# Four q offsets per load, 16 snapshot places, and node n at partition n/25 in a graph network on one Trainium2 core

## The chip, the cores and the metric

The program runs on one core of one Trainium2 chip as a single launch. The metric is device time in microseconds (us). TensorE (PE in the profile, PEld its weight loads), VectorE (DVE), ScalarE (ACT), GpSimd (POOL) and SyncE (SP) have instruction queues of their own and meet at semaphores. Three runs of the kernel before gave 8099.27, 8096.51 and 8084.9 us, median 8096.51.

## The reference

N = 3125 nodes with 128 features, E = 100,000 directed edges sorted by `dst`. Four stages, each added to its input and normalised:

```python
def _transformer_conv(x, src, dst, qw, qb, kw, kb, vw, vb, sw, sb):      # 8 heads of 16
    q, k, v = x@qw+qb, x@kw+kb, x@vw+vb                                   # (N, 8, 16)
    alpha = sum(q[dst] * k[src], -1) / sqrt(16)
    a = exp(alpha - segment_max(alpha, dst)[dst])
    a = a / segment_sum(a, dst)[dst]
    return segment_sum(v[src] * a[:, :, None], dst) + x @ sw + sb

L0: conv(relu(conv(x)))                                     # two such layers
L1: mean = segment_sum(x[dst], src) / max(deg(src), 1);  out = [x, mean] @ W.T + b
L2: h = x@W_enc; three times: m = relu(h[src] + ea) * edge_atten; sum by dst; two-layer MLP
L3: h = x@W.T + b; z = (h@a1)[src] + (h@a2)[dst]
    h' = segment_sum(exp(-leaky_relu(z, 0.2)) * h[dst], src); layernorm; elu
x = layernorm(x + Lk(x))   for each of the four
```

`deg(src)` is the number of edges with that source, and both sums of L1 and L3 go by `src`, against the order of the edges.

## The kernel before, in words

Node tensors live in SBUF as 128 partitions by 25 slots of 128 features (NT = 25, NP = 3200). Before the change node n sits at partition n % 128, slot n // 128.

**Preparation** (to about 163 us) makes lists: which node window each batch of edges belongs to, where each node's last partial sum stands (`last_item`), and for each source node which rows of the counting table it needs (`own_at`, from one-column products in line 504).

**conv_edges**, lines 595 to 830, runs once for each of the two layers of L0 (263 to 1747 us and 1961 to 3404 us). It has 208 batches a layer; a batch is 4 groups of 128 edges. It is software-pipelined: the iteration of batch t asks for the q rows of batch t+1 and finishes batch t-10 (`BEHIND`). On each engine a batch has:
- POOL: 4 gathers of k and v rows by edge (L622), into a ring of `SLOTS` places.
- PE: `ask`, which reads the q rows as a product of one-hot matrices with the q table in SBUF, 12 bf16 products (L696). Where in the q table each half of the batch starts is a number that PE reads from SBUF into a register first (`value_load`, L692), once for each half. Then `tally`, 704 counting products a layer (L702, up to four a batch), each added into PSUM bank 7; and the item products (L740), fp32, which sum weighted v rows and weights of batch t-10, two items of two products each.
- DVE: q times k (L783), v times weights (L788), head sums (L793), the weighted one-hot matrices (L796), evacuation of the items (L819), one-hot matrices for counting (L767, L772); every eighth batch the scans (L804 to L810).
- ACT: a snapshot (L661) of bank 7 after each tally, since each running count is wanted on its own, and a copy of the weights into the batch's `va` (L682), which the item products wait for.
- SP: writes the snapshots to `snap_tab` in DRAM, four at a time, and the items to `item_tab`.

A tally waits for the snapshot of the one before. PE's order in an iteration is tally, ask (load, six products, load, six products), tally, item, tally, item, tally; the last is followed by the first tally of the next iteration. ACT takes the first two snapshots of an iteration, then L682, then the other two.

**by_src**, lines 1447 to 1500, forms the sums by source for L1 (`x`, 3502 to 3726 us) and L3 (attention, 7730 to 8008 us). For each of 25 slots n of destination nodes POOL gathers two rows per partition of `snap_tab` (L1459, 128 x 3200 fp32, the count up to the end of a node's edges and the count up to its start), DVE subtracts them (L1468), in L1 sums them to in-degrees (L1477), in L3 takes the smaller of two exponentials (L1471) that ACT computes (L1487, L1489) and multiplies (L1474). PE then adds 25 products (L1496) with the counts as stationary operand and the features moving, 128 columns each, which leaves the sums node by partition.

**The rest**: GINE (L2's three layers, 3869 to 7656 us) is untouched. Linear layers go through `node_linear`. x comes in by two transfers (L208 24 slots, L210 the last 53 nodes), the output leaves by two more (L1598, L1599).

## Time and profile before

| | |
|---|---|
| runs | 8099.27, 8096.51, 8084.9 us |
| profiled execution, its own time | 8076.82 us |
| its span in the trace | 8075.1 us |
| mean granted PE clock | 0.591 |
| conv_edges, two layers | 1484.0 + 1443.0 us |
| by_src mean, by_src attention | 224 + 278 us |
| GINE | 3787 us |

The profile's page gives busy times by engine and by line; the windows view gives them for a stretch; the timeline lists instructions in order, with the idle time of the engine ahead of each in brackets and what ended it; the waits view sums those idle times. The granted clock is a share of the full 2.4 GHz.

### The profile page before, as it was taken

Reading aid. Unit: us, or ns where it says so; the run is one execution under the profiler, and the core shown is the slowest. Engines: PE = TensorE matmul, PEld = TensorE weight load, DVE = VectorE, ACT = ScalarE, POOL = GpSimd, SP = SyncE. Lnnn points to the kernel's source line nnn. Section 1 sums busy time; section 2 is a strip of 40 time slices with the busy share of each in tenths; the row PEclk is TensorE's granted clock in tenths of the full one; section 3 lists DMA queues with packets and bytes.
Section 4 is the critical chain, followed back from the end, with each engine's and each line's share of the span. In section 5 each row is a group of like instructions: output and inputs, shape, how many; then the busy total and the mean of one; then the engine's idle time right before and its main releaser. Section 6 shows DMA issues by size and latency. Waiting matters only on the chain. (4 is left out here: it accounts for less than half of the span.)

```text
span 8075.1 us, 75499 instructions
## 1 busy us (share of the span) xinstructions
PE 3659.2 (45%) x15737; PEld 2363.8 (29%) x15739; DVE 4330.2 (54%) x9443; ACT 866.8 (11%) x2809; POOL 4213.9 (52%) x4279
## 2 busy tenths in 40 slices
PE   4366666663666666655222322332322323322244
PEld 2254444442444444455110101111110101100144
DVE  5455555554555555576444444344444344544478
ACT  0011111110111111101000000000000000000043
POOL 0455555533555555410566666466666466666443
PEclk7555555565555555577556555565566665566677
DMA  1454555524555454364322222222222222222264
GB/s 30 138 147 141 145 149 145 146 79 122 149 145 145 142 148 140 109 258 168 100 85 87 88 85 87 69 89 85 87 87 85 70 87 85 90 86 87 65 238 187
DMA packets 571997, 943.76 MB, mean 117 GB/s; under 512 B 90581, under 2 KB 413611, under 8 KB 558680
## 3 DMA queue, kind: packets, MB, share of 16 engines
q0 software_dynamic: 173728, 545.15, 22.4%
q1 hardware_dynamic: 398008, 395.34, 15.7%
q8 instruction: 139, 2.28, 0.1%
q14 instruction: 122, 1.00, 0.0%
HBM read 619.47 MB, written 320.66 MB: 116 GB/s over the span
## 5 line engine op out<-in xcount | busy, mean ns | idle before, releaser
L1199 POOL DMA_INDIRECT big<-h_tab,big x2352 | 2237.8, 951 | 1420.0 <-issue 799.3
L622 POOL DMA_INDIRECT big<-kv_tab,big x1664 | 1617.4, 972 | 1330.7 <-DVE big L788 867.6
L1235 PE MATMUL psum<-big 128*128 128x512 f32 x1176 | 969.8, 973 | 2505.4 <-DVE big L1263 2062.1
L1256 DVE SCALAR_TENSOR_TENSOR big<-big 128x128 f32<-128x128 f32 x2352 | 827.2, 352 | 1274.0 <-issue 1233.8
L1235 PEld LDWEIGHTS psum<-big 128*128 128x128 f32 x1176 | 308.5, 290 | 3013.9 <-issue 2253.8
L740 PE MATMUL psum<-big 128*128 128x136 f32 x3328 | 931.4, 433 | 488.8 <-issue 417.1
L740 PEld LDWEIGHTS psum<-big 128*128 128x128 f32 x3328 | 781.9, 315 | 642.2 <-issue 605.1
L696 PE MATMUL psum<-big 128*128 x4992 | 713.3, 296 | 408.9 <-issue 408.7
L1268 DVE TENSOR_SCALAR big<-big 128x128 f32<-128x128 f32 x2352 | 718.0, 306 | 311.3 <-issue 261.8
L783 DVE TENSOR_TENSOR big<-psum,big 128x512 f32<-128x512 f32 x416 | 287.5, 691 | 851.9 <-PE psum L696 554.9
L702 PE MATMUL psum<-big 128*128 128x128 bf16 x1408 | 577.7, 410 | 216.1 <-ACT big L661 112.6
L696 PEld LDWEIGHTS psum<-big 128*128 128x128 bf16 x4992 | 454.2, 120 | 711.6 <-issue 671.7
L661 ACT COPY big<-psum 125x128 f32<-125x128 f32 x1408 | 376.3, 267 | 2444.5 <-PE psum L702 1517.0
L1263 DVE TENSOR_TENSOR big<-psum,big 128x512 f32<-128x512 f32 x588 | 404.3, 688 | 299.7 <-issue 199.7
L1220 ACT COPY big<-psum 128x128 f32<-128x128 f32 x294 | 77.9, 265 | 3312.5 <-issue 1555.2
L1459 POOL DMA_INDIRECT big<-snap_tab,small x100 | 215.3, 2153 | 397.1 <-DVE big L1468 218.3
L819 DVE SCALAR_TENSOR_TENSOR big<-big,psum 128x136 f32<-128x136 f32 x832 | 294.5, 354 | 204.0 <-PE psum L740 81.7
L702 PEld LDWEIGHTS psum<-big 128*128 128x128 bf16 x1408 | 227.4, 161 | 306.8 <-issue 258.5
L788 DVE TENSOR_TENSOR big<-big 128x512 f32<-128x512 f32 x416 | 284.1, 683 | 0.5 <-ACT big L669 0.5
L796 DVE TENSOR_TENSOR big<-big,small 128x512 f32<-128x512 f32 x416 | 284.2, 683 | 0.0
L793 DVE TENSOR_REDUCE big<-big 128x32 f32<-128x512 f32 x416 | 282.8, 680 | 0.7
L1496 PE MATMUL psum<-skip,big 128*128 128x128 f32 x1250 | 183.7, 320 | 110.3 <-DVE big L1474 110.3
(374 smaller groups left out, 3359.9 us busy)
## 6 DMA issues: line engine op xcount, KB each, us to landing
run_tab<-big SPq DMA_DIRECT2D x294, 512.0 KB
snap_tab<-big SPq DMA_DIRECT2D x352, 224.0 KB
item_tab<-big SPq DMA_DIRECT2D x208, 272.0 KB
big<-loc_tab SPq DMA_DIRECT2D x104, 512.0 KB
big<-h_tab,big POOLq DMA_INDIRECT x2352
big<-kv_tab,big POOLq DMA_INDIRECT x1664
snap_tab<-big SPq DMA_DIRECT2D x352, 26.0 KB
kv_tab<-big SPq DMA_DIRECT2D x10, 640.0 KB, 3.3
```

What stands on the lines that cost most here:

```text
L622: nc.gpsimd.indirect_dma_start(out=kv[:, b % SLOTS, k, :], out_offset=None, in_=kv_tab, in_offset=bass.IndirectOffsetOnAxis(ap=src_item[:, ...
L661: nc.scalar.copy(snaps[0:125, n % 8 * P:(n % 8 + 1) * P], bank[7][0:125, 0:P]).then_inc(snapped, 1)
L696: ins_ = nc.tensor.matmul(bank[b % 2][:, k * P:(k + 1) * P], hot_T[b // 4 % 2][:, (b % 4 * 4 + k) * P:(b % 4 * 4 + k + 1) * P], q3[:, bass ...
L702: nc.tensor.matmul(bank[7][:, 0:P], key_hot[n // 8 % 2][:, n % 8::8], lo_hot[n // 8 % 2][:, n % 8::8], start=first_c + n == 0, stop=True, ...
L740: ins_ = nc.tensor.matmul(region(2 * b + i), hot[b % 2][:, k * P:(k + 1) * P], va[b % 2][:, k, :], start=s == 0, stop=s == 1)
L783: nc.vector.tensor_tensor(prod[t % 2].rearrange("p (k c) -> p k c", c=D), bank[t % 2][:, :].rearrange("p (k c) -> p k c", c=D), kv[:, t % ...
L819: nc.vector.scalar_tensor_tensor(run[:, i % 8, :], run[:, (i - 1) % 8, :], keep[:, i:i + 1], region(i), ALU.mult, ALU.add).then_inc(run_do ...
L1199: nc.gpsimd.indirect_dma_start(out=ring[:, slot * D:(slot + 1) * D], out_offset=None, in_=h_tab, in_offset=bass.IndirectOffsetOnAxis(ap=sr ...
L1235: nc.tensor.matmul(bank[2 * u + k][:, :], ea_T[u], w_blocks[:, k * 512:(k + 1) * 512], start=True, stop=True).then_inc(mm_done, 1)
L1256: nc.vector.scalar_tensor_tensor(run[:, slot * D:(slot + 1) * D], run[:, (slot - 1) % RUN * D:((slot - 1) % RUN + 1) * D], same_nat[:, bas ...
L1263: nc.vector.tensor_tensor(z_of(u), bank[u][:, :], ring[:, u * 512:(u + 1) * 512], ALU.add).then_inc(z_done, 1)
L1268: nc.vector.tensor_scalar(m_of(u)[:, k * D:(k + 1) * D], z_of(u)[:, k * D:(k + 1) * D], 0.0, weight_nat[:, bass.ds(16 * i + 4 * u + k, 1)] ...
```

## The change

1. PE reads four q offsets at once, once in two batches (L702), without the bounds instructions, and applies them as offsets of a slice.
2. PE's order is tally, half of ask, tally, other half of ask, tally, item, tally, item.
3. `snaps` has 16 places for 8, is written out eight at a time; `SLOTS` is 14 for 15.
4. Node n is at partition n // 25, slot n % 25. A partition's 25 nodes are neighbours in DRAM: tables are written and read as rows of one partition, x and out as 96 + 29 partitions of 12.8 KB. The lists are made to match.
5. In this layout the count up to the start of a node in slot n is the count up to the end of its neighbour in the slot before; `own_at` has 30 columns and by_src makes 30 gathers for 50, into nine buffers.
6. by_src's products are turned: features stationary, counts moving, 512 columns at a time, seven for 25. A new `turn_back` brings the sums back to node by partition (25 products, 25 DVE operations, after copies from PSUM by ACT and DVE). L1's linear part on x moves ahead of by_src, the part on the mean goes into `turn_back`.
7. In L1 the subtraction also sums (one DVE pass for two). In L3 DVE takes the smaller exponent ahead of one Exp on ACT, and the product takes `min(…, 3e38)` in the same pass.

```diff
-SLOTS = 15
+SLOTS = 14
-        snaps = take(8 * P)
+        snaps = take(16 * P)
-        own_at = small[:, 330:330 + 2 * NT].bitcast(I32)
+        own_at = small[:, 330:330 + NT + 5].bitcast(I32)
         def table(t, cols=None):
-            return t.rearrange("(t p) c -> p t c", p=P)
+            return t.rearrange("(p t) c -> p t c", t=NT)
...
-                    sp.dma_start(x3[:, 0:NT - 1, :], a["x"][0:(NT - 1) * P, :].rearrange("(t p) d -> p t d", p=P)).then_inc(loads, 16)
+                    rows = a["x"].rearrange("(p t) d -> p (t d)", t=NT)
+                    sp.dma_start(x[0:96, :], rows[0:96, :]).then_inc(loads, 16)
                     sp.wait_ge(cleared, 1)
-                    sp.dma_start(x3[0:TAIL, NT - 1, :], a["x"][(NT - 1) * P:N, :]).then_inc(loads, 16)
+                    sp.dma_start(x[96:NODES_P, :], rows[96:NODES_P, :]).then_inc(loads, 16)
...
-                        def ask(b):
-                            pe.wait_ge(hotT_done, b // 4 + 1)
-                            later(pe, prod_done, b - 1)
-                            for i in range(2):
-                                at = nc.tensor.value_load(q_at[0:1, 2 * b + i:2 * b + i + 1], min_val=0, max_val=(NWIN - 1) * 3 * D)
+                        def windows_of(b):
+                            return nc.values_load_multi_w_load_instructions(q_at[0:1, 2 * b:2 * b + 4], engines=(mybir.EngineType.PE,), min_val=0, max_val=(NWIN - 1) * 3 * D,
+                                                                            skip_runtime_bounds_check_because="the list of windows is capped when it is made")[1]
+                        def ask(b, i, at):
...
                             if t + 1 < BATCHES:
-                                ask(t + 1)
+                                ask(t + 1, 0, at[(t + 1) % 2 * 2])
                             for n in turn[1:2]:
                                 tally(n)
+                            if t + 1 < BATCHES:
+                                ask(t + 1, 1, at[(t + 1) % 2 * 2 + 1])
...
+                            for n in turn[2:3]:
+                                tally(n)
                             b = t - BEHIND
...
                                     if i == 0:
-                                        for n in turn[2:3]:
+                                        for n in turn[3:]:
                                             tally(n)
-                            for n in turn[2 if b < 0 else 3:]:
-                                tally(n)
+                            if t % 2 == 0 and t + 2 < BATCHES:
+                                at = windows_of(t + 2)
...
-                        for n in range(NT):
-                            later(pool, diff, n - 1)
-                            for k, rows in enumerate((upto_own, upto_last)):
-                                nc.gpsimd.indirect_dma_start(out=rows[n % 2], out_offset=None, in_=snap_tab,
+                        for v in range(NT + 5):
+                            later(pool, mm_done, v - R + 1)
+                            at = NT + v if v < 5 else v - 5
+                            nc.gpsimd.indirect_dma_start(out=counts[v % R], out_offset=None, in_=snap_tab,
...
-                            for a_ in range(NT):
-                                ins_ = nc.tensor.matmul(bank[a_ // 4][:, (a_ % 4) * D:(a_ % 4 + 1) * D], own[n % 3][:, a_ * P:(a_ + 1) * P], feat[:, n * D:(n + 1) * D],
+                            for lo in range(0, NP, 512):
+                                ins_ = nc.tensor.matmul(psum[:, lo:min(lo + 512, NP)], feat[:, n * D:(n + 1) * D], counts[n % R][:, lo:min(lo + 512, NP)],
...
+        def turn_back(per_tile, after):
...
+                    def _(act):
+                        for k in range(0, BANKS, 2):
+                            at = slice(512 * k, min(512 * (k + 1), NP))
+                            nc.scalar.copy(agg_T[:, at], psum[:, at]).then_inc(lifted, 1)
...
+                        for t in range(NT):
+                            per_tile(psum[:, t * D:(t + 1) * D], agg_T[:, t::NT]).then_inc(turned, 1)
...
-                sp.dma_start(out[0:(NT - 1) * P, :].rearrange("(t p) d -> p t d", p=P), x3[:, 0:NT - 1, :]).then_inc(out_done, 16)
-                sp.dma_start(out[(NT - 1) * P:N, :], x3[0:TAIL, NT - 1, :]).then_inc(out_done, 16)
+                sp.dma_start(out.rearrange("(p t) d -> p (t d)", t=NT)[0:96, :], x[0:96, :]).then_inc(out_done, 16)
+                sp.dma_start(out.rearrange("(p t) d -> p (t d)", t=NT)[96:NODES_P, :], x[96:NODES_P, :]).then_inc(out_done, 16)
```

PE in one iteration of conv_edges, before: a tally (L702), then ask from its first load on, up to the second load. ISA rows are register arithmetic.

```order
378 L702 MATMUL psum<-big 128x128
379 L692 TENSOR_LOAD big
380 L692 ISA x2
381 L696 ISA
382 L696 MATMUL psum<-big 128x128
383 L696 ISA
384 L696 MATMUL psum<-big 128x128
385 L696 ISA
386 L696 MATMUL psum<-big 128x128 x4
387 L692 TENSOR_LOAD big
388 L692 ISA x2
389 L696 ISA
```

The same place after, where ask is L712, the tally L720 and the load of offsets L702: load, tally, first half of ask, tally, start of the second half.

```order
392 L702 TENSOR_LOAD big
393 L720 MATMUL psum<-big 128x128
394 L712 ISA
395 L712 MATMUL psum<-big 128x128
396 L712 ISA
397 L712 MATMUL psum<-big 128x128
398 L712 ISA
399 L712 MATMUL psum<-big 128x128 x4
400 L720 MATMUL psum<-big 128x128
401 L712 ISA
402 L712 MATMUL psum<-big 128x128
403 L712 ISA
```

The load stands ahead of the first tally, once in two batches, and a tally stands between the halves of ask.

PE in the same iteration, later, before: the last products of ask, then tallies and items (L740), and the load for the next batch.

```order
394 L696 MATMUL psum<-big 128x128 x4
395 L702 MATMUL psum<-big 128x128
396 L740 MATMUL psum<-big 128x136 x2
397 L702 MATMUL psum<-big 128x128
398 L740 MATMUL psum<-big 128x136 x2
399 L702 MATMUL psum<-big 128x128
400 L692 TENSOR_LOAD big
```

After, where items are L764:

```order
406 L712 MATMUL psum<-big 128x128 x4
407 L720 MATMUL psum<-big 128x128
408 L764 MATMUL psum<-big 128x136 x2
409 L720 MATMUL psum<-big 128x128
410 L764 MATMUL psum<-big 128x136 x2
411 L720 MATMUL psum<-big 128x128
```

The tally that stood behind the last item stands ahead of the first one; the first row of the last piece is the end of ask, the last row the first tally of the next iteration.

DVE in by_src of L1, before: a difference and a sum for each slot.

```order
2952 L1462 UNCONDITIONAL_BRANCH
2953 L1468 TENSOR_TENSOR big<-big 128x3200
2954 L1477 TENSOR_REDUCE small<-big 128x1
2955 L1468 TENSOR_TENSOR big<-big 128x3200
2956 L1477 TENSOR_REDUCE small<-big 128x1
2957 L1468 TENSOR_TENSOR big<-big 128x3200
```

DVE there after: one operation for each of the 25 slots, then the reciprocal of the degrees.

```order
2981 L1495 UNCONDITIONAL_BRANCH
2982 L1516 SCALAR_TENSOR_TENSOR big,small<-big 128x3200 x25
2983 L1486 UNCONDITIONAL_BRANCH
2984 L1010 UNCONDITIONAL_BRANCH
2985 L1572 TENSOR_SCALAR big<-small 128x25
2986 L1573 RECIPROCAL big<-big 128x25
```

Two passes over 3200 elements are one. On SP the transfers of x at the start (L208, L210 before, L211, L213 after) and of the output at the end change their shapes. Before:

```order
0 L206 UNCONDITIONAL_BRANCH
1 L208 DMA x<-in_x 128x24x128
2 L210 DMA x<-in_x 53x128
3 L192 UNCONDITIONAL_BRANCH
4 L259 UNCONDITIONAL_BRANCH
```

After:

```order
0 L208 UNCONDITIONAL_BRANCH
1 L211 DMA x<-in_x 96x3200
2 L213 DMA x<-in_x 29x3200
3 L194 UNCONDITIONAL_BRANCH
```

The second transfer has 29 rows of 3200 numbers for 53 of 128.

## Rows read from the trace of the kernel before

**Rows 1.** The page: its head.

```profile
span 8075.1 us, 75499 instructions
```

**Rows 2.** Windows view, two layers: us, busy by engine, PEclk, DMA share, GB/s.

```profile
263.00:1747.00 1484.00, 979.92 (x4968) 705.80 (x4968) 840.62 (x1553) 234.77 (x990) 770.09 (x794) 0.53 0.49 139
1961.00:3404.00 1443.00, 964.16 (x4905) 696.06 (x4902) 831.81 (x1540) 232.93 (x983) 748.32 (x772) 0.53 0.49 140
```

**Rows 3.** The page's costliest groups of conv_edges: busy, mean ns, idle before, releaser.

```profile
L622 POOL DMA_INDIRECT big<-kv_tab,big x1664 | 1617.4, 972 | 1330.7 <-DVE big L788 867.6 <-issue 463.1
L740 PE MATMUL psum<-big 128*128 128x136 f32 x3328 | 931.4, 433 | 488.8 <-issue 417.1
L696 PE MATMUL psum<-big 128*128 x4992 | 713.3, 296 | 408.9 <-issue 408.7
L783 DVE TENSOR_TENSOR big<-psum,big 128x512 f32<-128x512 f32 x416 | 287.5, 691 | 851.9 <-PE psum L696 554.9
L702 PE MATMUL psum<-big 128*128 128x128 bf16 x1408 | 577.7, 410 | 216.1 <-ACT big L661 112.6
```

**Rows 4.** PE's queue, line 692: duration min/median/max in ns.

```profile
L692 PEldq TENSOR_LOAD <-big x832: 294/302/1601, 262.3 to 3367.0; - x167
L692 PEldq FUSED_REGOPS  x832: 151/151/709, 262.9 to 3367.3; - x167
```

**Rows 5.** Timeline, an undisturbed batch from 1009.41 us.

```profile
1009.41 0.41 PE L702 MATMUL psum<-big 128*128 128x128 bf16 x1
1010.29 0.85 PE L696 MATMUL psum<-big 128*128 x6 [0.47 <-issue]
1011.32 0.86 PE L696 MATMUL psum<-big 128*128 x6 [0.17 <-issue]
1012.91 1.25 PE L740 MATMUL psum<-big 128*128 128x136 f32 x4 [0.52 <-issue]
1015.07 0.41 PE L702 MATMUL psum<-big 128*128 128x128 bf16 x1
```

**Rows 6.** Timeline, later batches in which PE stood before an item or a tally.

```profile
1026.14 1.25 PE L740 MATMUL psum<-big 128*128 128x136 f32 x4 [2.78 <-issue]
1029.16 0.40 PE L702 MATMUL psum<-big 128*128 128x128 bf16 x1 [0.45 <-ACT big L661]
...
1046.27 1.02 PE L740 MATMUL psum<-big 128*128 128x136 f32 x3 [2.58 <-ACT big L682]
```

**Rows 7.** Windows view, by_src of L1 and of L3, columns as in rows 2.

```profile
3530.00:3720.00 190.00, 147.10 (x1122) 142.72 (x1122) 159.25 (x46) 0.00 (x0) 39.32 (x42) 0.91 0.95 378
7760.00:7980.00 220.00, 153.97 (x1061) 149.78 (x1060) 219.27 (x65) 126.95 (x44) 153.25 (x43) 0.84 0.82 318
```

**Rows 8.** Timeline: start of by_src in L3.

```profile
7730.06 0.94 POOL L1459 DMA_INDIRECT big<-snap_tab,small  x1 [101.37 <-issue]
7741.28 3.49 DVE L1468 TENSOR_TENSOR big<-big 128x3200 f32<-128x3200 f32 x1 [20.76 <-DMA big<-snap_tab,small]
```

**Rows 9.** Timeline: one 512-column fp32 product at the lower and at the full clock.

```profile
7630.00 2.08 PE L1402 MATMUL psum<-big,bias 128*128 128x512 f32 x2 [13.34 <-ACT big L1379]
7638.46 1.12 PE L1402 MATMUL psum<-big,bias 128*128 128x512 f32 x2 [0.84 <-ACT big L1379]
```

**Rows 10.** Windows view: two-source linear of L1, one-source linear of L2.

```profile
3726.00:3763.00 37.00, 21.76 (x150) 20.25 (x150) 11.20 (x28) 13.49 (x30) 0.00 (x0) 0.82 0.02 6
3785.00:3811.00 26.00, 15.72 (x75) 13.50 (x75) 6.85 (x26) 6.99 (x15) 0.00 (x0) 0.61 0.02 5
```

**Rows 11.** The group of conv_edges' item evacuation on DVE.

```profile
L819 DVE SCALAR_TENSOR_TENSOR big<-big,psum 128x136 f32<-128x136 f32 x832 | 294.5, 354 | 204.0 <-PE psum L740 81.7 <-remote 47.4 <-issue 31.3
```

**Rows 12.** Windows view: x coming in, its tail, the output's tail.

```profile
2.60:7.60 5.00, 0.00 (x0) 0.00 (x0) 0.00 (x0) 0.00 (x0) 0.79 (x3) 1.00 0.98 279
8.80:9.30 0.50, 0.00 (x0) 0.00 (x0) 0.00 (x0) 0.00 (x0) 0.00 (x0) 1.00 0.07 22
8072.90:8074.30 1.40, 0.00 (x0) 0.00 (x0) 0.00 (x0) 0.00 (x0) 0.00 (x0) 0.50 0.07 18
```

More of the change, by code:

```diff
@@ L500, in _ @@
                     pe.wait_ge(to_pe, 3)
-                    for k, off in enumerate((5, 0)):
-                        for t in range(NT):
+                    for k, off, many in ((0, 5, NT), (1, 0, 5)):
+                        for t in range(many):
                             for b in range(CB):
-                                ins_ = nc.tensor.matmul(bank[6][:, k * NT + t:k * NT + t + 1], upto[:, b * DW + off + t * P:b * DW + off + (t + 1) * P], ones_bf[:, 0:1], start=b == 0, stop=b == CB - 1)
+                                ins_ = nc.tensor.matmul(bank[6][:, k * NT + t:k * NT + t + 1], upto[:, b * DW + off + t:b * DW + off + t + NT * (P - 1) + 1:NT],
+                                                        ones_bf[:, 0:1], start=b == 0, stop=b == CB - 1)
                     ins_.then_inc(from_pe, 1)
@@ L705, in _ @@
                         if layer > 0:
-                            nc.tensor.matmul(bank[7][:, 0:P], ident[:, :], snaps[:, 7 * P:8 * P], start=True, stop=True, skip_group_check=True)
+                            nc.tensor.matmul(bank[7][:, 0:P], ident[:, :], snaps[:, 15 * P:16 * P], start=True, stop=True, skip_group_check=True)
                         pe.wait_ge(q_in, 32)
-                        ask(0)
+                        at = windows_of(0)
+                        for i in range(2):
+                            ask(0, i, at[i])
                         for t in range(BATCHES + BEHIND):
@@ L872, in _ @@
                         if layer == 1:
-                            ins_ = nc.tensor.matmul(bank[3][:, 0:NT], snaps[:, 7 * P:8 * P], hi_pick, start=True, stop=True)
+                            ins_ = nc.tensor.matmul(bank[3][0:NT, 0:P], hi_pick, snaps[:, 15 * P:16 * P], start=True, stop=True)
                         ins_.then_inc(from_pe, 1)
@@ L1129, in _ @@
                         ins_.then_inc(from_pe, 1)
[L1130 to L1131 removed]
+                        nc.tensor.matmul(bank[6][:, 0:1], upper[:, :], in_all[:, 0:1], start=True, stop=True).then_inc(from_pe, 1)
                     @block.vector
@@ L1469, in _ @@
+                        if attention:
+                            smaller(0)
+                        for n in range(NT):
+                            own, upto = counts[n % R], counts[(n + 5) % R]
+                            if attention and n + 1 < NT:
+                                smaller(n + 1)
+                            if n < 5:
+                                dve.wait_ge(cin[n], 16)
+                            dve.wait_ge(cin[(n + 5) % R], 16 * ((n + 5) // R + 1))
                             if attention:
-                                dve.wait_ge(e_ready, 2 * n + 2)
@@ L1475, in _ @@
                             else:
-                                dve.wait_ge(diff, n + 1)
-                                nc.vector.tensor_reduce(edges_of[:, n:n + 1], u, AX_X, ALU.add).then_inc(in_degree, 1)
-                        dve.wait_ge(mm_done, NT)
-                        if not attention:
-                            dve.wait_ge(in_degree, NT)
+                                nc.vector.scalar_tensor_tensor(own, upto, 1.0, own, ALU.mult, ALU.subtract, accum_out=edges_of[:, n:n + 1]).then_inc(diff, 1)
@@ new lines, in build, with per_degree @@
+        node_linear([x[:, :]], [(wgt[:, 0:D], a["L1_WT"][0:D, :]), (wgt[:, D:2 * D], a["L1_WT"][D:2 * D, :]), (bias[:, 0:D], a["L1_b"].to_broadcast([P, D]))],
+                    D, [(skip[:, :], D, 0, D)], [])
+        by_src(x, False)
+        inv_deg = s12[:, 0:NT]
+        def per_degree(link, on_act):
+            link(nc.vector.tensor_scalar(inv_deg, deg, 1.0, None, ALU.max))
+            link(nc.vector.reciprocal(inv_deg, inv_deg))
+        node_math(per_degree, [])
+        turn_back(lambda to, of: nc.tensor.matmul(to, of, wgt[:, D:2 * D], start=True, stop=True),
+                  lambda t: nc.vector.scalar_tensor_tensor(skip3[:, t, :], psum[:, t * D:(t + 1) * D], inv_deg[:, t:t + 1], skip3[:, t, :], ALU.mult, ALU.add))
```

196 lines of the change are left out of this document (112 added, 84 removed).

## The prediction

> **What bounds the kernel now.** I read the page first for the size of the parts, then the windows of each stage, then, for the largest part touched, the groups, the waits and two timelines. The span is 8075.1 us [rows 1]; the profiled execution's own time is 8076.8 us and the median of the runs shown 8096.5 us, 20 us (0.24%) above. I sum against 8076.8 and add the 0.24% at the end. GINE, 47% of the span, is not touched. The two conv_edges layers take 1484 + 1443 = 2927 us for 416 batches [rows 2], so 7.13 us for the first layer's mean batch (1484/208). No engine fills a batch. PE is busy 980/208 = 4.7 us, DVE 4.0 us. POOL's four gathers take 4 x (0.97 + about 0.30 between them) = 5.1 us, and they stood idle 867.6 us behind DVE's L788 [rows 3]: POOL could run faster and is held by the ring, so by DVE. DVE in turn waits for PE: 554.9 us before L783 for ask's products [rows 3]. So a batch is a ring of PE, ACT and DVE in which PE is the one that the others wait for most, and PE's own idle time (in front of ask 408.9, items 488.8 and tallies 216.1 us, 1114 us in all [rows 3], 2.7 us a batch) is what can be recovered. PE runs in it at a granted clock of 0.53 [rows 2], near its lower level of 1.2 GHz.
>
> by_src of L1 is different: the DMA share is 0.95 at 378 GB/s [rows 7], so its 50 loads set the time. by_src of L3 is bound by DVE, busy 219 of 220 us [rows 7] with three passes of 3.49 us a slot.
>
> **conv_edges, the q offsets.** Each load takes 0.30 us on PE's queue and the register work behind it 0.15 [rows 4], 0.45 together, twice a batch. The gap that they leave: from the end of the tally (1009.82) to the first half of ask (1010.29) 0.47 us, and between the halves 0.17 us visible in the modelled ends [rows 5]; counting from the last weight load of one group to the first of the next, I put the two at about 0.5 us each, since a matmul queued while PE's sequencer is loading also starts late. After, one load serves two batches and costs 0.30/2 = 0.15. Gain 0.3 to 1.0 us a batch; I take 0.85 with the load's own 0.15 off.
>
> **conv_edges, the tallies and items.** Two adjacent tallies make PE wait for ACT's snapshot (0.45 us in the disturbed batch at 1029.16 [rows 6], 112.6 us in all [rows 3], 0.27 a batch); now there is half an ask or an item between any two, 0.8 to 1.1 us of PE, which covers the snapshot. The items wait for L682, which on ACT stands behind the second tally's snapshot; they stood idle 0.52 us in an undisturbed batch [rows 5] and 2.6 to 2.8 us in a disturbed one [rows 6], 488.8/416 = 1.17 us on average [rows 3]. The second tally now comes half an ask earlier, so its snapshot and L682 do too, and another tally (0.41 us [rows 5]) fills the gap ahead of the items. Against it: a third tally now stands before the item, and its wait for snapshot two is in front of the items. I take 0.45 us off here and 0.25 for the adjacent tallies. The edit could also give nothing, where the disturbed batches stay, since these are held by DVE and not by PE's order.
>
> Sum a batch: 0.85 + 0.45 + 0.25 = 1.55, so 7.13 goes to about 5.6 us. What is late next is POOL at 5.1 us, hence no lower than that; the undisturbed batch of rows 5 took 5.66 us (1009.41 to 1015.07) and shows that 5.6 is within reach once disturbances shrink. 1.53 x 416 = **−636 us**. Bounds: −844 (T = 5.1) and 0.
>
> The ring of 14 for 15 costs nothing while POOL waits for DVE; its price is in the rivals. Snapshots written eight at a time halve the number of writes from SP, which has room (DMA share 0.49 [rows 2]): 0.
>
> **by_src of L1.** Before, 224 us. After, 30 loads for 50: at 1.638 MB and 378 GB/s a load is 4.3 us, 130 us in all, so the DMA is no longer the end. DVE has one pass of 3.49 for two, 87 us. PE is the bound: 3200 columns a slot. One 512-column product took 2.08 us at the lower clock and 1.12 us at the full one [rows 9]; the difference of 0.96 is its columns at full clock, the rest fixed and hidden when they queue. 6.25 x 0.96 = 6.0 us a slot; the 50 records a slot of before at 0.131 us and clock 0.91 [rows 7] come to the same. The clock was 0.91 in this stage and PE will be busier, so I take 6.0: 150 us. The start needs six loads: in L3 the first two were there 11.2 us after the first issue [rows 8], so six after 11.2 + 4 x 4 = 27, and 3.5 for DVE. 27 + 3.5 + 150 = 181, **−43**. At the lower clock it would be 331, +107.
>
> **L1's linear part.** Before, 37 us for mean and two-source linear [rows 10]. After, a one-source linear (26, L2's [rows 10]), 1 for the degrees, PSUM copied by two engines (3 to 4), 25 products each followed by a DVE operation on 128 columns out of PSUM, 0.35 each by the nearest [rows 11], 9, and some 7 for block changes and waits: 47. **+10** (bounds +2, +16).
>
> **by_src of L3.** DVE keeps three passes of 3.49 a slot, so 10.4 us a slot stay. PE needs 6.0 at full clock and 12 at the lower; its clock of 0.84 [rows 7] gives 7.2, under DVE. The start waits for six loads for two, +16, less the two smaller-of passes done meanwhile, 7: **+9**. turn_back: 3 to 4 for the copies, 25 x 0.30, less the reduction of 3.5 that it saves: **+9** with its latencies. The way there loses a transpose and a copy and gains two passes of 1.7 us: **−3**.
>
> **x in and out.** The second transfer of x has 53 rows and its tail ran at DMA share 0.07, which is 1/16, at 22 GB/s, while the first moved 279 GB/s; the output's tail has 0.07 again at 18 GB/s [rows 12]. Now 29 rows of 12.8 KB, 371 KB, stand in its place. At 22 GB/s that is 17 us for the 27 KB's 1.2. At the start it begins about where it did, +12; at the end most of the write of before remains under it, +10: **+22**. If it spread over all engines it would be 371 KB at 279 GB/s, 1.3 us, and the term 0. The Trainium skill ("DMA: Bandwidth & Descriptors", "Why a DMA increments its semaphore by 16 and not by 1") says that such a transfer uses the largest number of engines up to 16 that divides its outermost count: one for 53 and one for 29, all 16 for 96 and 128. The trace agrees with it on the 53 rows (0.07 of 16).
>
> **The lists.** L504 goes from 350 to 210 one-column products, but with weights at a stride of 25 elements, which no row shows; bounds −4 and +25 us, taken 0. The added DVE operations on 25 columns and the degrees' way through DRAM stand beside conv_finish's gathers: 0.
>
> Sum: −636 − 43 + 10 + 9 + 9 − 3 + 22 = −632. 8077 − 632 = 7445, and with 0.24% more **7463 us** for the median.
>
> **Rivals.**
> 1. *Forecast*, T between 5.3 and 6.1 us: 7320 to 7650. Chance 0.54.
> 2. *POOL's pace.* PE is denser, its clock rises above 0.53, and each of its durations shrinks until only the gathers are left, T = 5.1. For it: gathers come 1.25 us apart as soon as a slot is free; against it: 4.7 us of PE in 7.1 did not raise the clock so far. −844 for −636: 7254. Chance 0.17.
> 3. *Half of it comes.* The idle time of PE that I take from the loads was a shadow of waits on DVE and ACT (the 2.6 to 2.8 us before items [rows 6] stay). T = 6.4: 0.73 x 416 = −304, and −300 in all: 7796. Chance 0.24.
> 4. *The change doesn't do what it says.* T stays 7.13 and only the small terms are left, +4: 8100. Chance 0.02.
> 5. *Slower: the shorter ring.* If a batch is set by the time a gathered row needs from its issue to L788's use of it, T goes with 1/SLOTS: 7.13 x 15/14 = 7.64, +212, in all 8077 + 216 plus 0.24%: 8313. It decides from the point where DVE's L783 or L788 waits on a gather; in the rows DVE waits for PE's L696 [rows 3]. Chance 0.03.
>
> With any of them the lower clock may hold in by_src of L1, +150 us on the forecast: 7610, inside the range. I give this 0.15.
>
> **How the numbers follow.** The likeliest is 7463, alone 7320 to 7650. The range for 8 in 10 cuts rival 2 and rival 3 at their middle: 7250 to 7800. A difference under 0.2% (16 us) can't be told from no change here. Faster: 0.54 + 0.17 + 0.24 = 0.95; same 0.02; slower 0.03.
>
> **What would show it.** PE's three loads per batch-pair fewer, idle time in front of ask's products below 0.3 us a batch for 1.0 (408.9/416); in front of the tallies no wait on L661; T in the windows of both layers 5.3 to 6.1; POOL's gathers near 1.25 us apart with less idle behind L788; by_src of L1 at PE's pace with DMA share below 0.8; x's tail of 17 us at share 0.07. The forecast is wrong if DVE's L783 still idles over 1.5 us a batch for PE, if the items' mean wait of 1.17 us stays, or if a wait on kv_tab appears on DVE.

## The result and the profile after

The kernel after takes 7883.35 us (median of 7881.1, 7901.74, 7883.13 and 7883.57), the kernel before 8090.7 us beside it: a ratio of 0.9748, 95% interval 0.973 to 0.9767, so 2.5% faster. The forecast was 7463 us, with a range of 7250 to 7800: the sign is right, the step forecast is three times too large. The profiled execution after took 7881.1 us, its span 7879.4, that is 195.7 us less than the span before [rows 1].

The page's head after:

```profile
span 7879.4 us, 68763 instructions
```

Where the 195.7 us are, by the timelines of both traces (a layer from its first product on DVE to its last evacuation of items):

| stretch | before | after | change | forecast |
|---|---|---|---|---|
| start to the first product of layer 0 | 271.9 | 283.2 | +11 | +12 |
| layer 0 | 1472.0 | 1378.9 | −93 | −318 |
| between the layers | 180.9 | 180.8 | 0 | 0 |
| layer 1 | 1477.5 | 1378.4 | −99 | −318 |
| from there to GINE's first gather | 467.2 | 409.2 | −58 | −33 |
| GINE and on to the first gather of by_src in L3 | 3860.6 | 3872.8 | +12 | −3 |
| from there to the end | 345.0 | 376.1 | +31 | +28 |

Every stage but conv_edges came within 25 us of its term. conv_edges brought 192 us for 636. The windows view of the first layer after and of by_src in L1 (columns as in rows 2), to set beside [rows 2] and [rows 7]; the second layer has the same granted clock of 0.66:

```profile
274.00:1665.00 1391.00, 818.94 (x4968) 677.59 (x4968) 834.96 (x1554) 231.40 (x990) 778.60 (x795) 0.66 0.51 148
...
3380.00:3500.00 120.00, 120.00 (x315) 55.95 (x314) 75.19 (x45) 0.00 (x0) 37.48 (x21) 1.00 0.78 291
```

by_src of L1 is as forecast: PE busy all the time, at full clock, DMA share 0.78 for 0.95. In the first layer PE's busy time shrank from 980 to 819 us, with the granted clock at 0.66 for 0.53, and yet the layer is only 6% shorter. The page's groups of conv_edges after, the answer to [rows 3] (L635 was L622, L764 L740, L720 L702, L712 L696, L809 L783, L674 L661):

```profile
L635 POOL DMA_INDIRECT big<-kv_tab,big x1664 | 1628.2, 978 | 1158.3 <-DVE big L814 694.9
L720 PE MATMUL psum<-big 128*128 128x128 bf16 x1408 | 568.7, 404 | 926.6 <-ACT big L674 498.1
L764 PE MATMUL psum<-big 128*128 128x136 f32 x3328 | 800.8, 401 | 201.1 <-DVE big L845 122.1
L809 DVE TENSOR_TENSOR big<-psum,big 128x512 f32<-128x512 f32 x416 | 286.8, 690 | 777.0 <-remote 627.0
L712 PE MATMUL psum<-big 128*128 x4992 | 613.1, 276 | 106.1 <-issue 105.9
L674 ACT COPY big<-psum 125x128 f32<-125x128 f32 x1408 | 375.8, 267 | 2100.0 <-remote 1081.4
```

The idle time ahead of ask fell from 408.9 to 106.1 us and that ahead of the items from 488.8 to 201.1, as forecast. The idle time ahead of the tallies rose from 216.1 to 926.6: it has moved. Taken together PE's idle time ahead of these three groups did not fall at all, 1113.8 us before and 1233.8 after; their busy time fell, by 240 us. PE now waits ahead of the tallies for ACT's snapshot, and ACT and DVE wait with the releaser "remote". That means that the semaphore was updated at the moment they woke, but that the instruction that should have updated it had ended long before, by the trace. The timeline after shows such a place:

```profile
1000.86 0.40 PE L720 MATMUL psum<-big 128*128 128x128 bf16 x1 [3.06 <-issue]
...
1001.08 0.55 PE L712 MATMUL psum<-big 128*128 x6
1002.09 0.95 POOL L635 DMA_INDIRECT big<-kv_tab,big  x1 [0.30 <-issue]
1004.73 0.27 ACT L674 COPY big<-psum 125x128 f32<-125x128 f32 x1 [4.02 <-remote]
1004.86 0.69 DVE L809 TENSOR_TENSOR big<-psum,big 128x512 f32<-128x512 f32 x1 [4.99 <-remote]
...
1005.14 0.40 PE L720 MATMUL psum<-big 128*128 128x128 bf16 x1 [3.51 <-ACT big L674]
```

The tally starts at 1000.86 and lasts 0.40 us, its snapshot has nothing else to wait for, and starts 3.87 us later (0.45 us is the usual distance). The last products of ask start before 1001.5, and DVE, which waits for them, starts at 1004.86. Both hand-overs from PE are late and come together. The trace records the updates of the semaphores too: the tally's stands at 1004.71 and that of ask's last product, which started at 1001.41, at 1004.78. So it is not ACT or DVE that wake late. The update comes late, though whether the product itself ended late is not told, since the ends of PE's products are modelled.

I call a release late where a snapshot starts over 1.5 us after its tally. Paired over 1390 tallies (the first nine of a layer left out) the trace of before has 116 (312 us from tally to snapshot), that of after 375 (1196 us). A snapshot can also be late because ACT was busy with something else. The stricter count is of tallies whose own semaphore update stands 1.5 us or more behind their start: 84 before and 323 after (212 and 992 us from start to update). That is where the gain went. The expectation of e1 below gives the first count as 117 and 376, and 284 and 1045 us, by an earlier pairing.

### The profile page after: what moved, and what is told of

Its sections match the earlier page's. It is cut to its first block and busy times, and to the rows that moved or that the text cites. A ratio compares the mean times of both kernels' runs of the same rounds, so it can differ in the third digit from the quotient of the medians.

```text
span 7879.4 us, 68763 instructions
## 1 busy us (share of the span) xinstructions
PE 3359.0 (43%) x13794; PEld 2133.8 (27%) x13796; DVE 4251.2 (54%) x9506; ACT 783.0 (10%) x2777; POOL 4134.4 (52%) x4239
## 5 line engine op out<-in xcount | busy, mean ns | idle before, releaser
L635 POOL DMA_INDIRECT big<-kv_tab,big x1664 | 1628.2, 978 | 1158.3 <-DVE big L814 694.9
L1268 PE MATMUL psum<-big 128*128 128x512 f32 x1176 | 997.3, 997 | 2493.0 <-DVE big L1296 1779.6
L1268 PEld LDWEIGHTS psum<-big 128*128 128x128 f32 x1176 | 312.8, 294 | 3022.3 <-issue 2483.6
L720 PE MATMUL psum<-big 128*128 128x128 bf16 x1408 | 568.7, 404 | 926.6 <-ACT big L674 498.1
L764 PE MATMUL psum<-big 128*128 128x136 f32 x3328 | 800.8, 401 | 201.1 <-DVE big L845 122.1
L764 PEld LDWEIGHTS psum<-big 128*128 128x128 f32 x3328 | 690.6, 290 | 260.0 <-issue 214.6
L809 DVE TENSOR_TENSOR big<-psum,big 128x512 f32<-128x512 f32 x416 | 286.8, 690 | 777.0 <-remote 627.0
L712 PE MATMUL psum<-big 128*128 x4992 | 613.1, 276 | 106.1 <-issue 105.9
L674 ACT COPY big<-psum 125x128 f32<-125x128 f32 x1408 | 375.8, 267 | 2100.0 <-remote 1081.4
L712 PEld LDWEIGHTS psum<-big 128*128 128x128 bf16 x4992 | 467.1, 120 | 195.1 <-issue 112.2
L720 PEld LDWEIGHTS psum<-big 128*128 128x128 bf16 x1408 | 209.5, 149 | 1064.9 <-issue 1004.4
L1492 POOL DMA_INDIRECT big<-snap_tab,small x60 | 124.0, 2067 | 466.5 <-PE psum L1531 276.4
L1531 PE MATMUL psum<-big,skip 128*128 128x512 f32 (+1 forms) x350 | 179.8, 676 | 133.7 <-DVE big L1514 133.7
```

What stands on the lines that cost most here:

```text
L635: nc.gpsimd.indirect_dma_start(out=kv[:, b % SLOTS, k, :], out_offset=None, in_=kv_tab, in_offset=bass.IndirectOffsetOnAxis(ap=src_item[:, ...
L674: nc.scalar.copy(snaps[0:125, n % 16 * P:(n % 16 + 1) * P], bank[7][0:125, 0:P]).then_inc(snapped, 1)
L712: ins_ = nc.tensor.matmul(bank[b % 2][:, k * P:(k + 1) * P], hot_T[b // 4 % 2][:, (b % 4 * 4 + k) * P:(b % 4 * 4 + k + 1) * P], q3[:, j * ...
L720: nc.tensor.matmul(bank[7][:, 0:P], key_hot[n // 8 % 2][:, n % 8::8], lo_hot[n // 8 % 2][:, n % 8::8], start=first_c + n == 0, stop=True, ...
L764: ins_ = nc.tensor.matmul(region(2 * b + i), hot[b % 2][:, k * P:(k + 1) * P], va[b % 2][:, k, :], start=s == 0, stop=s == 1)
L809: nc.vector.tensor_tensor(prod[t % 2].rearrange("p (k c) -> p k c", c=D), bank[t % 2][:, :].rearrange("p (k c) -> p k c", c=D), kv[:, t % ...
```

## The experiments

Layers are the sum of both as in the table above. "Late" is the first count, and in brackets the stricter one, of late updates. Runs taken together on one chip, with the kernel before among them, are a session here (the expectations say call); ratios are within a session. One fact has to be told first. The kernel before takes 7971 to 8099 us in some sessions and 7136 to 7163 us in others (but for a single run of 7873 us in the session of e5 to e8), and one chip gave either at different times. I call these the long and the short level. What sets the level stays open. No session at the long level but the first has a trace of before, so layers and counts are compared across sessions there.

| run | level of before | ratio to before (95%) | layers | late (late updates) |
|---|---|---|---|---|
| before, after (first pair) | long | 0.9748 (0.973 to 0.9767) | 2950, 2757 | 116 (84), 375 (323) |
| e1 loads only | long | 0.9911 (0.9895 to 0.9928) | 2860 | 219 (172) |
| e2 order only | long | 0.9930 (0.9907 to 0.9953) | 2864 | 350 (247) |
| e3 snapshots and ring only | long | 0.9946 (0.993 to 0.9963) | 2880 | 95 (90) |
| e4 after with old loads | long | 0.9808 (0.9792 to 0.9825) | 2785 | 314 (275) |
| e13 after, fixed offset | long | 0.9680 (0.9648 to 0.9711) | 2715 | 406 (351) |
| e14 after, half the bytes | long | 0.9743 (0.9714 to 0.9771) | 2747 | 380 (324) |
| e15 after, half the gathers | long | 0.8527 (0.8498 to 0.8556) | 1780 | 69 (0) |
| e16 after, kv by SP | long | 0.8506 (0.848 to 0.8531) | 1774 | 67 (0) |
| e17 before | short | 1.0004 (0.9992 to 1.0015) | 2680 | 35 (0) |
| e5, e9 after | short | 0.9216 (0.9198 to 0.9233), 0.9208 (0.9193 to 0.9224) | 2139, 2142 | 72, 68 (0) |
| e6, e10 after, fixed offset | short | 0.9203 (0.9185 to 0.922), 0.919 (0.9175 to 0.9206) | 2138, 2139 | 72, 69 (0) |
| e7, e11 after, half the bytes | short | 0.9218 (0.9201 to 0.9234), 0.9212 (0.9196 to 0.9227) | 2145, 2148 | 63, 64 (0) |
| e8, e18 after, old order | short | 0.9236 (0.9219 to 0.9254), 0.9241 (0.9204 to 0.9278) | 2157, 2158 | 4, 4 (0) |
| e12 after, rows split | short | 0.9179 (0.9164 to 0.9195) | 2136 | 69 (0) |

**e1 to e4: the parts of the change in conv_edges.** e1 is the kernel before with

```diff
-                                at = nc.tensor.value_load(q_at[0:1, 2 * b + i:2 * b + i + 1], ...)
+                        at = windows_of(t + 2)      # four values, once in two batches, as in after
```

> The kernel before with the q offsets loaded four at a time and nothing else. After the change, 376 snapshots of ACT started over 1.5 us after their tally (1045 us in all), for 117 (284 us) before; these late releases took what the shorter PE work gave. Theory L (the loads pay, the new order of the tallies brings the late releases): PE's idle time ahead of ask falls by some 0.8 us a batch, late releases stay near 117, a batch falls from 7.0 to 6.2 us or less and the time by 250 to 350 us, so the load alone beats the whole change. Theory D (a denser PE and denser gathers bring the late releases, whatever edit made them denser): late releases rise to 200 or more, the time falls by under 150 us. Theory N (a load's time lay in waits anyway): within 30 us of before.

e2 is the kernel before with `ask(t + 1, 0)`, tally, `ask(t + 1, 1)`, tally, items as in after, and a `value_load` in each half.

> The kernel before with the tallies and halves of ask in the order of after (one register load for each half, as before). Theory L: late releases rise above 300, most behind the tally that stands between the halves of ask; the batch stays at 7 us or gets longer, time 0 to +150 us. Theory D: late releases stay under 200 since PE is no denser, the time falls by 50 to 150 us as the wait between adjacent tallies goes.

e3 is the kernel before with

```diff
-SLOTS = 15
+SLOTS = 14
-        snaps = take(8 * P)
+        snaps = take(16 * P)
-                                if n % 4 == 3:
+                                if n % 8 == 7:
```

> The kernel before with 16 snapshot places written eight at a time and 14 places in the ring of gathered rows, nothing else. Theory S (a snapshot transfer twice as long holds up the gathers and the releases): late releases rise above 200 and the time grows by 50 us or more. Theories L and D: within 20 us of before, late releases near 117.

e4 is the kernel after with one `value_load` in each half of ask.

> The kernel after with one register load for each half of ask, everything else as after. Theory L: the time grows by 250 us or more against after, late releases stay above 300. Theory D: late releases fall towards 150 and the time grows by under 100 us against after.

Measured: 7908.8, 7913.9, 7931.4 and 7822.6 us for 7975.5 before. Each part alone earns 44 to 67 us, 173 us together, and no one of them carries the change. e1 came out as theory D has it: the loads alone are worth 67 us and bring 219 late releases for 116. Its trace shows why so little: idle time ahead of ask is down to 106.2 us, just as in after, but that ahead of the items is up from 488.8 to 828.5. e2 has 350 late releases and is 62 us faster all the same, so neither the theory that the order costs time nor the one that late releases need a denser PE holds. Here the items' idle time is down to 194.0 us and that of the tallies up to 680.9. e4 fits neither theory: 314 late releases are more than theory D has, and a ratio of 0.9808 for the 0.9748 of after, some 50 us across two sessions, is far less than theory L has. e3 was expected at no change and gave 44 us: in the trace of before ACT waits 110.9 us, 28 times, for a snapshot transfer before it may overwrite a place, and in e3 it has no such wait. I had priced the 16 places at nothing. e3 changes the ring and the places together, so no run has the price of the ring alone.

**e5 to e8: the level turns out to matter.**

> The kernel after, unchanged, as the base for the others of this call on the same chip. All theories: 2.3 to 2.7% under before, two layers' first-to-last products about 1348 us each, some 375 late releases (a snapshot over 1.5 us after its tally's start).

e6 has no register in the address: `q3[:, j * D:(j + 1) * D]` for `q3[...][:, bass.ds(at, D)]`, and no load.

> After, with ask reading the q table at a constant place: no register load, no register in the address; the same products on other data, so only the values differ. Theory R (late releases come from the register loads or from addresses by register, which hold PE up when the DMA is busy): late releases fall below 100 and a batch to 5.6 us or less, -350 us against after. Theory D (dense PE work under dense DMA traffic, whatever the addresses): late releases stay above 300; the time falls by under 100 us against after.

e7 leaves out the v half of each row: `out=kv[:, b % SLOTS, k, 0:D], in_=kv_tab.rearrange("n (h d) -> (n h) d", h=2)`.

> After, with each gathered row of kv 512 bytes for 1024 (the v half of the ring is filled once with a constant), so half the gathered bytes and as many gather instructions. Theory D: late releases fall below 150, batch towards 5.6 us, -300 us or more against after. Theory R: late releases stay above 300 and the time within 60 us of after.

e8 is after with PE's old order and the loads four at a time.

> After, with PE's order of tallies, halves of ask and items as before (the loads stay four at a time). If the order is what brings the late releases, they fall from 375 to about 220 (what the load alone had) and the time falls under after; if the order earns its 53 us of the run with the order alone, the time grows by 30 to 80 us against after.

Here before took 7147.3 and after 6583.9 us, 7.8% less, where I expected 2.3 to 2.7%. The layers of after take 2139 us for 2757, a batch (their 416th part) 5.14 us. The windows view of the first layer of e5 and the groups of both:

```profile
270.00:1348.00 1078.00, 774.20 (x4968) 627.40 (x4968) 832.52 (x1554) 231.13 (x990) 785.43 (x798) 0.74 0.66 193
```

```profile
L635 POOL DMA_INDIRECT big<-kv_tab,big x1664 | 1641.7, 987 | 534.6 <-issue 499.9
...
L809 DVE TENSOR_TENSOR big<-psum,big 128x512 f32<-128x512 f32 x416 | 286.5, 689 | 411.6 <-DMA big<-kv_tab,big 372.1
```

POOL's gathers now follow one another (of 534.6 us idle 499.9 are the pause between instructions) and DVE waits 372.1 us for their data: a gather comes every 1.29 us ((1641.7 + 499.9)/1664), so four take 5.15 us, which is the batch. Since e6 and e7 change nothing at that pace (6581.6 and 6590.5 us), they tell only that the loads, the addresses and half the bytes are hidden there; e8 (6601.2 us) tells that the new order is worth 17 us, and e18 repeats it (6607.7 us). 68 to 72 late releases are left, and in none of them is PE's update late: 52 are by design, since once in eight batches the third tally's snapshot stands behind ACT's Exp.

**e9 to e12: the same again, and the row transfers.**

> After, unchanged, as the base of this call. On the chip of the first pair it won 2.5% and had 375 late releases; on the chip of the second call, where before took 7147 us, it won 7.8% with 72. Both theories: where before takes some 8000 us here, late releases are above 300 and the win is 2 to 3%; where before takes some 7150 us, as in the second call.

> After with ask at a constant place of the q table (no register load, no register in the address; values differ). On the chip where before took 7147 us it changed nothing (6582 for 6584 us). On a chip where before takes some 8000 us: theory R (instructions whose address comes from a register are what stalls) expects late releases below 100 and a batch below 5.8 us, -300 us against after; theory D (any hand-over is late while the DMA is busy) expects above 300 and within 100 us.

> After with half the bytes in each gathered row (the v half is a constant). Without effect where before took 7147 us (6590 for 6584 us). On a chip where before takes some 8000 us: theory D expects a batch under 6 us and late releases under 200; theory R no change within 60 us.

e12 is after with

```diff
-                    sp.dma_start(x[96:NODES_P, :], rows[96:NODES_P, :]).then_inc(loads, 16)
+                    for lo, hi in ((96, 112), (112, 120), (120, 124), (124, 125)):
+                        sp.dma_start(x[lo:hi, :], rows[lo:hi, :]).then_inc(loads, 16)
```

and the same for the output.

> After with the last 29 partitions of x and of the output as four transfers of 16, 8, 4 and 1 partitions. The prediction priced the 29-row transfer at +12 us in and +10 us out because it runs on one DMA engine. Then the first product of conv_edges comes 8 to 12 us earlier and the stretch from the last gathers to the end gets 6 to 10 us shorter; if the transfer's engines were no cause, neither moves by over 2 us.

Once more the short level (before 7155.5, after 6591.1 us), where e10 and e11 (6576.0 and 6592.0 us) can't decide between the theories. e12 took 6565.5 us, 25.6 less than after beside it. SP's timeline of after (the first pair) and of e12:

```profile
4.30 0.29 SPq L213 DMA_DIRECT2D x<-in_x  x1
24.32 0.83 SPq L269 DMA_DIRECT2D big<-in_dst  x2
```

```profile
4.30 1.32 SPq L214 DMA_DIRECT2D x<-in_x  x4
15.58 0.83 SPq L270 DMA_DIRECT2D big<-in_dst  x2
```

The next transfer starts at 15.58 for 24.32 us (24.45 in e9, beside e12). From e9 to e12 the first product of conv_edges comes 10.6 us earlier, and the stretch from the last by_src's first gather to the end falls from 376.2 to 366.9 us, both as expected; they make 20 of the 25.6 us. While the 29 rows are under way in after (14 to 20 us) the DMA share is 0.07, about one engine of 16. e12 beats both kernels.

**e13 and e14: the long level again.** The same kernels as e6 and e7.

> After with ask at a constant place of the q table, for the third time, in search of a chip on which before takes some 8000 us. There theory R (instructions addressed by a register are what stalls) expects a ratio to before of 0.93 or less and under 100 late releases; theory D (any hand-over is late under DMA traffic) expects 0.965 to 0.98 and above 300. Where before takes 7150 us: 0.919 and about 70, and nothing is told apart.

> After with half the bytes in each gathered row, likewise. Where before takes some 8000 us theory D expects a ratio of 0.94 or less and under 200 late releases; theory R 0.97 to 0.98 and above 300. Where before takes 7150 us: 0.921.

This time before took 8078.2 us, e13 7819.4 and e14 7870.4. e13's 406 late releases end theory R: addresses by register don't make releases late. e14's 380 end theory D as far as it goes by bytes: half the gathered bytes change nothing. e13's ratio is 0.7% under that of the first pair, so at the long level the loads and registers cost some 50 us; that compares two sessions.

**e15 and e16: the gather instructions.** e15 is after with `for k in (0, 2)` for `for k in range(4)`. e16 takes the gathers off POOL:

```diff
-                                nc.gpsimd.indirect_dma_start(out=kv[:, b % SLOTS, k, :], out_offset=None, in_=kv_tab, ...)
+                                sp.dma_start(kv[:, b % SLOTS, :, :], kv_tab[512 * (b % 6):512 * (b % 6 + 1), :].rearrange("(p k) c -> p k c", k=4))
```

> After with two of the four gathers of each batch (the other two groups of the ring hold a constant). Theory G (the gather instructions and their descriptors, not their bytes, make hand-overs late): on a chip where before takes some 8000 us the late releases fall from about 380 to under 200 and the two layers shorten by 250 us or more; theory C (late releases belong to the chip and to PE's density, not to the gathers): above 300, under 100 us. On a chip where before takes 7150 us a batch was at the gathers' pace of 5.1 us: with half of them it falls to 4.5 to 4.8 us, so the floor behind POOL is DVE's 4.0 us plus its waits.

> After with the kv rows of a batch fetched by one plain transfer from SP's queue for POOL's four gathers (the same bytes, rows in order, values differ). Theory G: as in the run before, and more: late releases under 150 where before takes some 8000 us, a batch under 5.5 us. Theory C: above 300. On a 7150 us chip: a batch of 4.4 to 4.8 us.

Before took 8055.8 us here, e15 6873.4 and e16 6856.4. Late releases fell to 69 and 67, late updates to none, the layers to 1780 and 1774 us, a batch to 4.28 and 4.26 us. The windows view of the first layer in e15 and in e16:

```profile
270.00:1165.00 895.00, 719.42 (x4944) 567.02 (x4944) 814.58 (x1542) 230.73 (x989) 384.41 (x388) 0.84 0.59 171
```

```profile
270.00:1165.00 895.00, 721.09 (x4985) 568.22 (x4986) 819.12 (x1556) 231.57 (x990) 0.00 (x0) 0.85 0.77 236
```

DVE is busy 815 and 819 of 895 us. e16 moves 236 GB/s for the 148 of after, the same kv bytes in each batch. Apart from the 52 by design and the tallies between the items, 315 were late in after and 10 are in e16, as few as with the short level in e12's trace (11).

One rival had to be looked at: that these two profiled executions had slipped to the short level. They had not. GINE, which neither edit touches, tells the level by one row (more on it below). In e15 and in e16:

```profile
L1290 DVE SCALAR_TENSOR_TENSOR big<-big 128x128 f32<-128x128 f32 x2352 | 824.6, 351 | 1210.7 <-issue 1148.7
```

```profile
L1287 DVE SCALAR_TENSOR_TENSOR big<-big 128x128 f32<-128x128 f32 x2352 | 823.6, 350 | 1330.9 <-issue 1278.5
```

Over 1200 us of idle time are the long level; at the short one it is 22 us in e5. So at the long level it is POOL's gathers, by their number and not by their bytes, that make PE's updates late. This is shown for conv_edges, by two runs of each kernel in one session. e15 halves the gather instructions and the rows that they fetch together, so which of the two counts is open. By what path they delay PE's update is not shown either, nor why much denser gathers at the short level delay none.

**e17 and e18: before at the short level, and the order again.**

> The kernel before, unchanged, for a trace of its own. If before takes some 7150 us in this call: the two layers take about 2610 us (2882 less the 270 us that the other stages don't explain of the 944 us between the two levels), a batch 6.3 us, and late releases under 40; so the change's step in conv_edges is then about 6.3 to 5.1 us. If it takes some 8000 us: 2850 to 2900 us and some 116 late releases, as in the first trace. Theory G holds in both.

> After with PE's order as before, for the second time. Where before took 7147 us it lost 17 us to after and had 4 late releases. Where before takes some 8000 us: if the order brings the late releases, about 220 of them and the time 20 to 60 us under after (ratio 0.968 to 0.972); if it earns what it did alone (62 us), ratio 0.98 and more.

e17 took 7152.7 us, its span 7138.4. Its layers take 2680 us, for 2610 expected; 35 releases are late, none by a late update. Against e5 (2139) the change is worth 541 us in conv_edges at this level. e18 took 6607.7 us (ratio 0.9241, 0.9204 to 0.9278); what the order does at the long level with everything else as after stays open. The page has one row that shows the level in a part of the program that the change does not touch, GINE's sums on DVE; first in the trace of before of the first pair, then in e17:

```profile
L1256 DVE SCALAR_TENSOR_TENSOR big<-big 128x128 f32<-128x128 f32 x2352 | 827.2, 352 | 1274.0 <-issue 1233.8
```

```profile
L1256 DVE SCALAR_TENSOR_TENSOR big<-big 128x128 f32<-128x128 f32 x2352 | 826.2, 351 | 27.2 <-DVE big L1268 0.8
```

The same 2352 instructions, equally long, stand idle 1274 us at the long level, 1234 of them behind nothing that the profile shows, and 27 us at the short one. Between the two traces of before conv_edges differs by 270 us and the rest of the program by 668.

## Why the prediction was wrong

**The step that failed** is "Sum a batch: 0.85 + 0.45 + 0.25 = 1.55, so 7.13 goes to about 5.6 us." It takes PE's idle times as independent costs, so that each one removed shortens the batch by its own length. Over the layers a batch went from 7.09 to 6.63 us (2950 and 2757 over 416), −0.46 for −1.53, which is 192 of the 636 us. The terms by themselves: the loads, priced at 0.85 us a batch, earned 0.16 in e1 (67 us); the order, priced at 0.45 + 0.25, earned 0.15 in e2 (62 us). The idle times that I summed did shrink where I said, by 303 us ahead of ask and 288 ahead of the items. In the full change they came back 710 us larger ahead of the tallies, where the sum had a gain of 0.25 us a batch, as waits for late updates of PE's semaphores. These grew from 212 to 992 us between start and update.

The warning was in rows that I had read. The timeline of before, just ahead of the first batch of [rows 6]:

```profile
1025.65 0.27 ACT L661 COPY big<-psum 125x128 f32<-125x128 f32 x1 [4.20 <-remote]
1025.68 0.69 DVE L783 TENSOR_TENSOR big<-psum,big 128x512 f32<-128x512 f32 x1 [4.03 <-remote]
```

The 2.78 us ahead of the item at 1026.14 is the wait for this, by way of L682 behind that snapshot, and the 2.58 us at 1046.27 is another such place. I called these batches disturbed and took an undisturbed one [rows 5] as proof that 5.6 us was "within reach once disturbances shrink", and had no reason why they should. That batch proves something else: it took 5.66 us in the kernel before, with both loads and the old order in it. What made the mean batch 7.1 us were the disturbed ones, and nothing in the edit was aimed at them. The median step from one product L783 to the next did fall, from 6.65 to 5.85 us; the late updates took the rest.

**The sum.** Three readings in it are off besides. 7.13 is the first layer's batch; the mean of both is 2927/416 = 7.04, which makes the term 39 us too large. The likeliest range of T, 5.3 to 6.1, gives 7338 to 7672 by the prediction's own sum, not 7320 to 7650. And the load of four was priced as one load of 0.30 us; it takes 1.0 us (995 ns at least), so 0.50 a batch and not 0.15. With the loads gone at the long level (e13) the idle time ahead of the tallies is as large as before, 938.8 for 926.6 us.

**The rivals.** "Half of it comes" gave 6.4 us and 7796 us and was the nearest; the measured time lies 87 us above it. Its mechanism, that the idle time from the loads was a shadow of other waits, is borne out by e1, where what left the front of ask came back ahead of the items. What it did not have is that these waits on DVE and ACT were late updates behind POOL's gathers and would grow. "POOL's pace" is what the short level shows: 5.1 us a batch, gathers in a row, clock at 0.74 for 0.55. There the change saved 559 us of span (7138.4 to 6579.3), 541 of them in conv_edges, near the 632 and 636 forecast. That is luck, not a confirmation: the batch went from 6.44 to 5.14 us there, not from 7.13 to 5.6, and ended at the bound of rival 2. The shorter ring showed no cost that any run can tell: e3, with 14 places, is 44 us faster, and at the short level POOL's own pace accounts for the whole batch. A wait on kv_tab did appear on DVE there (372.1 us), as the prediction's signs of being wrong have it.

**The other terms.** by_src of L1 with L1's linear part and the stages around them: −58 for −33. PE ran at full clock (1.00 from 3380 to 3500 us) as assumed, and the last sums ended 162 us after the first gather for the 181 forecast, since a slot took 5.3 us there (120 us for 315 records, 14 a slot) for the 6.0 assumed; the start waited 27.51 us for six loads, 27 forecast. Start +11 for +12, end +31 for +28, and e12 confirms the row transfer by taking it away. The L504 products: 14.3 us of PE for 9.5, inside the bounds of −4 to +25, taken 0. The snapshots, taken 0, are −44 in e3.

**The range** ended at 7800 because I let "half of it" be the pessimistic end. The bound of the sum itself, no gain in the loop, was 8100, and the profile had no row that excluded it.

## What to carry to other kernels

Idle times of one engine in a loop of several are not costs that can be summed: remove one and see in a trace whether the batch got shorter or the wait moved, as it did in e1 and e2. When a wait ends by "remote", look up when the semaphore was updated and when its producer should have ended. If the update itself is late, no better order of this engine will close the gap: price it as a constant that stays or grows, and ask which engine's work runs beside it each time. Before a forecast in a loop with POOL's gathers, count the late updates. The count shows where a gain can go, not how long the kernel will take: e2 has more of them than before and is faster. And measure at more than one time: the same pair of kernels gave 2.5% and 7.9%.

## What the runs showed of the hardware

- At the long level 375 of 1390 hand-overs from PE to ACT came over 1.5 us after the tally's start, 323 of them by a late update of PE's semaphore; with half as many gather instructions on POOL 69 and no late update, with the same bytes by SP's plain transfers 67 and none, with half the bytes by as many gathers 380 and 324. At the short level there are none in any trace, with gathers 1.29 us apart.
- The level is no property of one chip: the same chip gave before 7155.5 us in one session and 8055.8 us in another.
- A load of four q offsets takes 1.0 us on PE's queue (995 ns at least), one of a single offset 0.30: four singles (1.2 us) and one of four cost nearly the same in the load itself.
- A transfer of 29 rows of 12.8 KB holds up its successor until 24.3 us, as 16 + 8 + 4 + 1 rows until 15.6. The Trainium skill ("DMA: Bandwidth & Descriptors", "Why a DMA increments its semaphore by 16 and not by 1") gives one engine for 29 rows and 16, 8, 4 and 1 for the parts. The DMA share of 0.07 in after and the time of e12 agree.
